# Cross attention 0: VectorE's two norm applies placed behind the max over keys, ScalarE's exponential ahead of the second copy of turned weights

## The reference, cut to what matters

```python
x = _layernorm(x + _L0_attn_ref(x, ...))     # its output product x @ w_proj and the norm: "norm C"
x = _layernorm(x + _L0_xattn_ref(x, ctx, ...))                                          # "norm D"

def _L0_xattn_ref(query, key_value, Wq, bq, Wk, bk, Wv, bv, Wo, bo):   # 16 heads of 16, 77 keys
    q, k, v = heads(query @ Wq + bq), heads(key_value @ Wk + bk), heads(key_value @ Wv + bv)
    attn = jnp.clip(q @ k.T * 0.25, -10000, 10000)
    attn = jax.nn.softmax(attn, axis=-1)
    return (attn @ v) @ Wo + bo
```

## Time and profile before

| | us |
|---|---|
| median of 3 runs | 2463.09 (2459.82 to 2463.49) |
| the profiled execution | 2465.59 |
| its span in the profile | 2463.9 |
| mean granted clock of TensorE | 0.825 of 2.4 GHz |
| TensorE, VectorE, ScalarE, GpSimd busy | 1799.4, 1842.0, 1338.7, 871.7 |
| the loop's score stretch, first to last start of L1385 | 706.0 to 1055.2 |

### The profile page before, as it was taken

How to read it: one execution, slowest core, us unless ns; L and a number is a source line. 1 busy time by engine, 2 the same in 40 slices (tenths; PEclk the granted TensorE clock), 3 DMA queues, 4 the chain that set the end, 5 groups by cost and what they waited for, 6 DMA issues and landing times. The chain is left out here.

```text
span 2463.9 us, 36495 instructions
## 1 busy us (share of the span) xinstructions
PE 1799.4 (73%) x12157; PEld 1133.0 (46%) x12168; DVE 1842.0 (75%) x4628; ACT 1338.7 (54%) x3347; POOL 871.7 (35%) x921
## 2 busy tenths in 40 slices
PE   8849999999867877755545554867999999344554
PEld 4513333333346666644434442544767777133333
DVE  4678888888258888869999995534666665699998
ACT  2106666666523434421888888739888852233333
POOL 2510000000058677533333330003634633355553
PEclk9958999999868989867676765687999999566766
DMA  2011111111010000000000001000000000000000
GB/s 74 17 26 28 28 30 30 30 29 22 22 49 12 31 12 12 5 1 1 1 1 1 1 1 54 13 17 1 18 1 1 1 1 1 32 13 13 13 14 17
DMA packets 42808, 41.55 MB, mean 17 GB/s; under 512 B 16054, under 2 KB 34670, under 8 KB 42622
## 3 DMA queue, kind: packets, MB, share of 16 engines
q1 hardware_dynamic: 42622, 39.23, 5.9%
HBM read 22.03 MB, written 4.19 MB: 11 GB/s over the span
## 5 line engine op out<-in xcount | busy, mean ns | idle before, releaser
L763 ACT ACTIVATE ST<-ST,aexp 128x1 f32<-128x1 f32 x2046 | 582.7, 375 | 54.9 <-PEq L57 54.9
L597 ACT ACTIVATE PT<-PS 128x512 f32<-128x512 f32 x576 | 309.8, 597 | 220.8 <-PE PS L482 189.6
L558 DVE CUSTOM_DVE_ANT_0 junk<-PS,maskw 128x128 bf16<-128x128 f32 (+3 forms) x512 | 226.4, 486 | 34.5 <-PE PS L459 34.4
L459 PE MATMUL PS<-KT,QT 48*128 48x512 bf16 (+3 forms) x768 | 190.2, 352 | 54.1 <-DMA QT<-QS 33.0
L94 PE MATMUL PS<-ident,X 128*128 128x128 f32 x320 | 78.7, 334 | 188.5 <-DVE X L128 172.5
L94 PE MATMUL PS<-ident,j_t 128*128 128x128 f32 x320 | 77.0, 424 | 165.6 <-ACT j_t L1954 136.7
L561 DVE TENSOR_REDUCE MX<-PS 128x1 f32<-128x512 f32 x256 | 164.5, 684 | 28.2 <-PE PS L459 25.3
L501 PE MATMUL PS<-PT,VP 128*32 128x256 f32 (+1 forms) x2560 | 185.0, 371 | 0.0
L1715 PE MATMUL PS<-L_xattn_VW,l_pT 112*128 112x256 f32 x704 | 159.4, 382 | 9.3 <-DVE i_xb L1741 6.5
L123 POOL TENSOR_TENSOR n_rs<-n_ve,neghalf 128x1 f32<-128x1 f32 x96 | 110.3, 1166 | 153.1 <-DVE n_ve L118 153.1
L631 POOL TENSOR_SCALAR nm<-MX 128x16 f32<-128x16 f32 x32 | 6.5, 204 | 432.2 <-DVE MX L564 432.2
(11 more groups left out here) (314 smaller groups left out, 4479.7 us busy)
## 6 DMA issues: line engine op xcount, KB each, us to landing
KT<-KS SPq DMA_DIRECT2D x192, 32.0 KB, 2.0
QT<-QS SPq DMA_DIRECT2D x192, 32.0 KB, 2.0
xs<-in_x SPq DMA_DIRECT2D x8, 512.0 KB
cx<-in_x SPq DMA_DIRECT2D x32, 128.0 KB, 2.0
out<-j_xn SPq DMA_DIRECT2D x32, 128.0 KB, 1.7
QT<-NMT SPq DMA_DIRECT2D x192, 2.0 KB
f_raw<-in_L_ffn_w SPq DMA_DIRECT2D x2, 1024.0 KB, 5.4
j_raw<-in_L_ffn_w SPq DMA_DIRECT2D x2, 1024.0 KB, 5.1
```

The lines of the kernel that those rows point to most:

```text
L459: T.matmul(bank(u % 3)[:, 0:w * P], QT[i % R][rows, qt * P:(qt + 1) * P], KT[i % R][rows, k0 * P:(k0 + w) * P], start=True, stop=True).the ...
L558: V.tensor_tensor_reduce(junk[u % 3][:, 0:w * P], bank(u % 3)[:, 0:w * P], maskw[:, BANK - w * P:], 1.0, NEG, ALU.add, ALU.max, MX[i % 2][ ...
L597: C.activation(PT[n % 4][:, 2 * pr + e, 0:w], bank(3 + u % 3)[:, 0:w], ACT.Exp, scale=0.25).then_inc(e_done, 1)
L763: C.activation(self.ST[:, m, t:t + 1], self.ST[:, m, t - 1:t] if t else self.zero[:, :], ACT.Tanh, bias=self.BU[:, m, t:t + 1], scale=self ...
```

## The change

In VectorE's list the two applies of a slot, of norm C to tile c-1 and of norm D to tile o-1, stood first. Now they stand behind the max over keys (L1385) and ahead of the residual add of tile c. In ScalarE's list the exponential of the slot stood last. Now it stands ahead of the copy of the second piece of turned weights, behind the copies of the first piece and of the turned X. Waits, buffers and semaphores are unchanged.

```diff
@@ dve() of cross_layer0
             for j in range(LAST + 1):
                 p, sc, c, q, o = j - 5, j - 4, j - 1, j - 8, j - 6
-                if on(c - 1):
-                    nC.dve_apply(c - 1, X[:, c - 1, :], cx[(c - 1) % 3][:, :]).then_inc(c_xn, 1)
-                if on(o - 1):
-                    nD.dve_apply(o - 1, X[:, o - 1, :], xb[(o - 1) % 5][:, :]).then_inc(d_xn, 1)
                 if on(q):
                     V.wait_ge(d_xn, q + 1)
...
                 if on(sc):
                     V.wait_ge(d_clip, sc + 1)
                     V.tensor_reduce(mx[sc % 4][:, :], by_head(s[sc % 4][:, :]), AX.X, ALU.max).then_inc(d_mx, 1)
+                if on(c - 1):
+                    nC.dve_apply(c - 1, X[:, c - 1, :], cx[(c - 1) % 3][:, :]).then_inc(c_xn, 1)
+                if on(o - 1):
+                    nD.dve_apply(o - 1, X[:, o - 1, :], xb[(o - 1) % 5][:, :]).then_inc(d_xn, 1)
                 if on(c):
                     V.wait_ge(c_mm, c + 1)
@@ act() of cross_layer0
                     C.copy(xT[f % 2][:, :], bank(3)[:, 0:D]).then_inc(d_xT, 1)
+                if on(sc):
+                    C.wait_ge(d_sub, sc + 1)
+                    C.activation(s[sc % 4][:, :], s[sc % 4][:, :], ACT.Exp).then_inc(d_exp, 1)
                 if on(p):
                     C.wait_ge(d_ptr1, p + 1)
...
                     last.then_inc(d_qT, 1)
-                if on(sc):
-                    C.wait_ge(d_sub, sc + 1)
-                    C.activation(s[sc % 4][:, :], s[sc % 4][:, :], ACT.Exp).then_inc(d_exp, 1)
```

## The result

The changed kernel took 2468.07 us in the median (2465.19 to 2471.76), the kernel before on the same chip 2463.81 (2459.82 to 2468.36). The ratio is 1.002 with a 95% interval of 1.0012 to 1.0027: slower by 0.2%, some 4 us, where 8 us less were forecast. The profiled execution has a span of 2464.5 at a mean granted clock of 0.832. That is only 0.6 above the span before, because in this execution the score stretch begins 4 us earlier (first max at 701.95 against 705.97; 3.2 of them come from the self attention, which the change does not touch), and what follows the last max is 1.7 us shorter. From the first to the last max it takes 355.57 us against 349.24, and this is the loss.

A forecast was written before the change was run, and what follows sets the result against it. Bound: the loop of max, GpSimd's subtraction and powers, and VectorE's queue, 11.03 us a slot. Window gains of 12.8 less 4.5 for the lower clock gave 2457.3, and 2.5 less for the median 2455; range 2446 to 2469.

The forecast's parts named there:

- the second apply "at 1.2": VectorE, norm D's apply beside GpSimd's subtraction: taken to last 1.2 us, 0.4 more than now, between 0.40 and about 2.25.
- the +4.5 for the lower clock: TensorE partly at 1.2 GHz in the new loop: 0.94 us more in a sixth of 30 slots, 0.15 each.
- the loop of 10.90: Max, subtraction, exponential, second copy, weighted sum, scores, clip, max: 10.90 us a slot, deciding over VectorE's 10.3.
- Rival 2: VectorE's second apply held for GpSimd's whole subtraction: pace 11.3 us, +5 in sum, about 2468; chance 0.15.
- the 12.8 that the loop was to bring: Saving summed over the five windows of attention slots, before any loss to the lower clock: 12.8 us.
- The wait of 1.58: VectorE's wait for GpSimd's second power of the norms, 1.58 us, expected to go in every slot.
- the 0.10 taken for the port: Delay of GpSimd's subtraction while the first apply may hold the port: 0.10 us, between 0 and 0.4.
- rival 4: GpSimd's subtraction held by both applies: every slot 0.3 us longer, about 2464; chance 0.15.
- Scaling and copy: VectorE's quantizing meets GpSimd's two adds: +0.53 us for the scale's copy, an estimated +0.3 for the scaling.
- GpSimd's queue: Slots with a weight pass of 3.64 us: GpSimd's work takes 11.2 us before the next subtraction.
- Rival 3: TensorE's weighted sum falls on the lower clock after waiting for the copy: slower, 2469 to 2486; chance 0.15.
- rival 5: The new ScalarE loop is not reached; VectorE's 10.3 us sets the unburdened slots, some -26, 2437; chance 0.10.

The follow-up runs named there:

- experiment 3: Changed kernel with norm D's apply moved from behind the max to behind the reciprocal; 2464.4 us, ratio 0.9999 to the kernel before.
- experiment 5: Changed kernel with GpSimd's subtraction of the max issued as two instructions of eight heads; 2468.05 us in one execution.
- experiment 7: Changed kernel with the subtraction replaced by a slow one-input GpSimd pass (max, then add) over 1232 elements; 2574.8 us in one execution.
- experiment 8: Changed kernel with the subtraction replaced by a one-input max-and-add pass over only 1024 of the 1232 elements; 2531.91 us in one execution.
- experiment 4: Changed kernel with norm D's apply behind the reciprocal and the exponential last on ScalarE again; 2430.18 us, ratio 0.9867 to the kernel before.
- experiment 6: Changed kernel with the subtraction replaced by a one-input pass (times 1, plus 0) over 1232 elements; 2439.75 us in one execution.
- experiment 2: Kernel before with only ScalarE's exponential moved ahead of the second copy, both applies first as before; 2461.84 us, ratio 0.9996.

## Why the prediction was wrong

The forecast was 2455 and faster, and the kernel takes 2468.07. The step that failed is the second apply "at 1.2", in the part on VectorE: it measured 2.34. A second term, the +4.5 for the lower clock, was too small as well, and alone would have taken the gain.

**The second apply.** It was bounded by 0.40 and 2.25, and taken at 1.2 from an apply beside a pass of 1024 elements. It measured 2.34, the upper end and the 0.1 that the subtraction became longer. So VectorE's pace is 11.38, not 10.3, and above the loop of 10.90 that was to decide. Experiments 3 (0.32 elsewhere, and the loss gone) and 5 (half the instruction, half the hold) show it; experiments 7 and 8 show that the row chosen did not carry over to a pass of 1232 elements. It was the nearest row by engine and by line, but not by size or form, and it shows the pass at its beginning only. The trace of the kernel before had the rest of it:

```profile
741.36 3.64 POOL L705 TENSOR_SCALAR f_raw<-f_raw 128x1024 f32<-128x1024 f32 x1
741.42 1.13 DVE L128 TENSOR_SCALAR X<-cx,nC_mv,nC_rs 128x256 f32<-128x256 f32 x1 [2.52 <-POOL nC_rs L123]
...
744.02 1.13 DVE L159 TENSOR_SCALAR e_xq<-e_t 128x256 bf16<-128x256 f32 x1
```

The rounding of L159 starts 2.66 into the pass and lasts 1.13 instead of 0.28, to 0.15 behind the pass's end. So even under this pass VectorE was held to the end, if it came late. And the applies beside the adds, whose 0.81 and 0.82 the prediction reads as a cost, end 0.15 behind those adds too.

Rival 2 is what happened, given at "about 2468" with a chance of 0.15: its pace of 11.3 is 11.38, and its five windows (71.9, 101.7, 71.9, 56.5, 44) are 68.27, 103.79, 71.48, 57.45 and 44.87 here. The five add up to 345.9 against its 346.0, and that is partly luck: it missed that two slots of the first window have no norm D (-3.6), and the second window has 1.3 us for the reduction of L691, which neither it nor the forecast's 9 x 10.9 has. The first slot's 1.5, set at nothing without a reason, is in neither. The Trainium skill, page "SBUF — State Buffer", section "Who interferes with whom", says that VectorE in a two-port mode and GpSimd exclude each other for whole instructions. The traces agree for the subtraction (2.34), its halves (1.307) and the slow pass of 1232 elements (4.451); they do not for instructions that come early or in the middle of the one-input passes of 1024 elements (1.12 beside 2.78 us in the earlier trace rows, 1.126 beside 3.722 us). Weighing rule against row, the row was given too much: it contradicted the rule for another shape.

**The lower clock in the new loop.** This was +0.15 a slot. In experiment 3, where the loop decides, the 30 slots take 340.5 where the forecast's windows add up to 328.2: +12.3 in place of +4.5, which takes nearly all of the 12.8 that the loop was to bring. So with the second apply at 1.2 the result would, by this estimate, have been about no change, as experiment 3 was. The estimate charged 0.94 to a sixth of the slots from the earlier trace rows. In experiment 3 twelve of the 30 slots have a clock share of 0.85 or 0.86 and are longer than 11: eight lose 1.3 to 1.5, four 0.6 to 0.9. The scores alone, at 2.43, take 1.06 more, where the row had 1.46.

**What was right.** The wait of 1.58 went in every slot, and the first apply takes 0.40 ahead of the subtraction, but for six burdened slots in which the division is still running and it takes 0.48 to 1.27. The subtraction is 2.35 instead of 2.25, the 0.10 taken for the port, so rival 4 did not come. Scaling and copy cost 0.90 more, where 0.83 was taken; experiment 4 shows that this is a cost of the late quantizing and not of the new order as such. The loop of ScalarE adds up to 10.90 and is measured at 10.89 to 10.90 in experiment 3. GpSimd's queue binds in the slots with a pass of 3.64, at 12.03 to 12.09, where the forecast had 11.2 and rival 2 had 12.3. The second copy starts 3.59 behind the end of the max (3.7 forecast). Rival 3, the lower clock, is not the cause of the loss in the changed kernel, whose granted clock in the five windows is not below that of the earlier trace rows; rival 5 is excluded, for the copy starts behind the exponential (865.96 behind 864.83).

**What stayed open.** Why one-input passes of 1024 elements are open in the middle and those of 1232 are not, and where between them it changes. Whether two-input passes of 1024 elements hold an apply was not tried. The halves of 616 elements (apply of 1.307) and the quick pass of experiment 6 (1.305) fit a hold, since the apply ends 0.15 behind their ends and a passage took 1.12 to 1.13, but they lie too near to it to prove one. Experiments 5 to 8 rest on one execution each; the applies in each agree within 0.02 us over the slots (one of 1.161 in experiment 8 apart). Which slots fall on the lower clock was not explained either.

## What to carry to other kernels

Moving a short VectorE instruction behind one that starts a GpSimd pass costs as much as the pass lasts, if the pass holds it: 2.34 us for 0.32 of work. A row taken from another pass has to match in shape, in form and in how far into the pass the instruction starts. Look for a place in the queue where GpSimd stands or has small work (here behind the reciprocal). When two orders are changed at once, add up for each the loop that it closes; here the place of norm C was good, and only the kernels with norm D and the exponential placed otherwise bring the 34 to 40 us.

## What the runs showed of the hardware

VectorE's apply (128 x 256, one input), started up to 0.16 us behind the start of a GpSimd pass over 1232 elements, ended 0.15 us behind the pass's end at 2.35 and at 4.45 us, and likewise at 1.31. Started 1.72 into the pass of 4.45, the scaling was held as well, for 2.88 us.

A one-input pass over 1024 elements acts on VectorE at both of its ends. An instruction that starts in its first 0.2 us lasts until 1.2 to 1.3 us into the pass (1.12 to 1.21 for the apply, beside passes of 2.78 to 3.72 us). One that starts between 1.1 us into the pass and some 1.1 us ahead of its end takes its own time (the apply 0.40 at 1.1 in the kernel before, 0.32 at 1.9 in experiment 3). One that starts later is held to 0.15 behind the end: 1.13 for L159 at 2.66 into 3.64, 1.02 for the apply at 1.92 into 2.80 in experiment 3. For a two-input pass over 1024 elements there is one kind of case, with a two-input VectorE instruction: in the kernel before, L1547 starts 0.08 behind the pass of L1628 (1.91 us) and lasts 1.98, against 0.34 alone. So the number of elements alone does not free VectorE.

GpSimd's time for 1232 elements depends strongly on the operations: times 1 plus 0 takes 1.31 us, a subtraction of two inputs 2.25 (2.35 where an apply is still running as it starts), largest and plus 4.45. The granted clock of a window can differ by more than its work does: 785 to 1012 us showed 0.98 in experiment 2 and 0.91 in the kernel before, at nearly the same slots.
